# Windowed attention in an AdaLN block: full-array transposes of the probabilities, and a new order of the slot's stages on TensorE, VectorE and ScalarE

## Chip, core and metric

One NeuronCore of a Trainium2 chip runs the whole program in one launch. The metric is the device time of that launch in microseconds (us). The kernel before takes 1208.83 us, the median of 3 runs (1204.72 to 1213.89).

## What is computed

The input is x, 16 sequences of 512 tokens with 128 channels, float32. The part that the change touches is the attention half of the block:

```
h = _layernorm(x, axis=-1) * (1 + ca) + sa
x = x + ga * _L0_attn_ref(h, w_qkv, w_out)

# _L0_attn_ref: H, D, window_size = (16, 64, 32)
xn = rms_norm(x)
q, k, v = jnp.split(xn @ w_qkv.T, 3, axis=-1)     # then split in 16 heads of 64
q = apply_rope(q, cos, sin)
k = apply_rope(k, cos, sin)
attn = jnp.einsum('bhqd,bhkd->bhqk', q, k) * scale
mask = (q_pos >= k_pos) & (q_pos - k_pos <= window_size)
attn = softmax(where(mask, attn, NEG))
out = jnp.einsum('bhqk,bhkd->bhqd', attn, v)
return out.transpose(0, 2, 1, 3).reshape(B, T, H * D) @ w_out.T
```

The second half (a second modulated layer norm, a dense attention over the 16 sequences, a mixture of 8 experts with one expert per token, two more layer norms) is the function `phase2`. The change does not touch it.

## The kernel before, in words

Everything is float32. A projection with a weight is done as three matmuls in the type fp32r, on a high and a low part of both operands: high by high, low by high, high by low.

The attention half runs as a software pipeline over 128 items, 16 sequences ("blocks") times 8 pairs of heads. The loop variable `s` counts slots, 137 of them. In slot `s` each engine works on several items at once, each at another stage. The offsets are `LS, LE, LT, LV, LO, LY = 2, 3, 4, 5, 6, 9` (line 166): the stage with offset L handles item `s - L`. The order of the stages inside a slot is written out by hand for each engine, and each engine takes its instructions strictly in that order. Semaphores say when operands and buffers are ready.

In one slot of the kernel before, TensorE does in this order:

1. q and k of item s: six matmuls 128x512 (lines 322 to 324, twice), into the two banks `PJ`. This is "rope" in the plan of the banks.
2. Scores of item s-2 (line 336): for 8 windows of 64 queries and both heads, 64 queries by 96 keys, into the banks `SC`.
3. Transposes of the probabilities of item s-4 (line 351): 16 transposes of 64 queries by 96 keys, so that the keys lie on partitions, into the banks `TR`. Those of the queries on partitions 0 to 63 go to one bank, those of 64 to 127 to the other. The two kinds stand in turn.
4. Probabilities by values ("PV") of item s-5 (line 367), into the bank `OB`.
5. Once in a block: four transposes of the finished output `yt` (line 377), and in another slot four of the next block's normed input `xn` (line 287), both full 128x128.
6. Values of item s (lines 298 to 300): three matmuls 128x512.
7. Output projection of item s-6 (lines 392, 393, 395): three matmuls 128x512 that accumulate in the bank `ACC` over the 8 items of a block.

ScalarE does in a slot: 8 exponentials (line 681, item s-3, with row sums), two copies of the transposed probabilities to SBUF (`pT`, line 691, item s-4), the copy `oth` of the PV result (line 700, item s-5) and the copy `vn` of the values (line 713, item s). Once in a block it adds four squares (line 647, slot 3), four scalings (line 654, slot 5) and the copy `xh` (line 662, slot 6).

VectorE does four multiplications by cos and sin from PSUM (lines 511, 512, item s), 8 masked row minima of the scores (line 523, item s-2), a reciprocal (line 532, item s-3) and the low part `otl` of the PV result (line 549, item s-5). Once in a block it adds the copy `yt` (line 501), `x1` (line 542), `xl` (line 429), the statistics (lines 411, 416) and, at the end of slot 1, `centre` (line 423): four instructions `(x - mean) * rstd`, each 128x128.

GpSimd adds the two halves of rope (`qk`, line 615, item s-1) and multiplies the exponentials by the reciprocals (line 621, item s-3). In some slots it adds a part of the next block's layer norm (lines 574 to 594) or the residual (line 635). SyncE issues the DMAs that swap partitions for rope (`sw`, line 221, four in a slot) and that spread the values over the windows (`vw`, lines 231 to 234).

Two banks `PJ` are used in turn by rope (two uses in a slot), values, `xn` and `yt`. So the second rope projection of slot s+1 waits for `vn` of slot s, and the first one for the second pair of cos and sin products of slot s.

## Time and profile before

| what | value |
|---|---|
| median of 3 runs | 1208.83 us |
| the profiled execution's own time | 1204.72 us |
| its span | 1202.7 us |
| TensorE busy | 1070.0 us, 89% of the span |
| VectorE, ScalarE, GpSimd busy | 971.2, 928.0, 854.8 us |
| mean granted TensorE clock | 0.939 of full speed |

The profiled execution is the fastest of the three. The span runs from the first to the last instruction and leaves 2 us around it. Busy time of TensorE is modelled, since matmuls overlap, so the length of a stretch of matmuls is read from starts, not from the sum of their durations. Releasers are inferred from semaphores.

### The profile page before, as it was taken

What the parts mean: (1) busy time and instruction counts of PE and PEld (TensorE: products, weight loads), DVE (VectorE), ACT (ScalarE), POOL (GpSimd) and SP (SyncE); (2) the same over time, 40 slices, a digit from 0 to 9 for tenths busy, and PEclk for the clock granted to TensorE, in tenths of its full rate; (3) what the DMA queues carried; (4) which work ended last, traced back from release to release, by engine and by line L of the source; (5) the groups of instructions that cost most, each with busy time, mean ns of one, the idle gap of its engine ahead of it and who ended that gap; (6) DMA issues with size and microseconds to landing.
All of it is one profiled execution on the core that took longest, in us unless ns stands there. A gap on an engine that the chain in (4) does not pass through costs nothing. (4 is left out here: it accounts for less than half of the span.)

```text
span 1202.7 us, 51645 instructions
## 1 busy us (share of the span) xinstructions
PE 1070.0 (89%) x18513; PEld 861.0 (72%) x18513; DVE 971.2 (81%) x4190; ACT 928.0 (77%) x3404; POOL 854.8 (71%) x685
## 2 busy tenths in 40 slices
PE   4799999999999999999999999847998985399994
PEld 2577777777777777777777777725877774388883
DVE  6899998898998898989989986636887864278885
ACT  2799989999999899999899997926876753266662
POOL 2787877877878877878778776654566767157777
PEclk7999999999999999999999998969998976599997
DMA  6776766776766666667677667443242212676200
GB/s 198 207 182 166 179 171 165 179 178 171 180 171 168 178 167 171 177 162 185 171 172 183 161 162 186 105 136 130 64 127 98 76 69 107 193 199 177 85 32 31
DMA packets 111034, 181.01 MB, mean 150 GB/s; under 512 B 19726, under 2 KB 64177, under 8 KB 110656
## 3 DMA queue, kind: packets, MB, share of 16 engines
q1 hardware_dynamic: 102944, 158.53, 51.1%
q0 software_dynamic: 6400, 16.82, 3.9%
q8 instruction: 152, 2.49, 0.9%
q10 hardware_dynamic: 1440, 2.36, 0.8%
q14 instruction: 98, 0.80, 0.2%
HBM read 35.20 MB, written 24.73 MB: 50 GB/s over the span
## 5 line engine op out<-in xcount | busy, mean ns | idle before, releaser
L615 POOL TENSOR_TENSOR qk<-mm,sw 128x1024 f32<-128x1024 f32 x128 | 306.2, 2392 | 127.9 <-DMA sw<-mm 127.7
L681 ACT ACTIVATE pr<-sm,mn 128x96 f32<-128x96 f32 x1024 | 368.0, 364 | 1.0 <-DVE mn L523 1.0
L511 DVE TENSOR_TENSOR mm<-bank,cos 128x512 f32<-128x512 f32 x256 | 174.8, 683 | 47.9 <-PE bank L324 40.9
L621 POOL TENSOR_TENSOR pr<-pr,ri 128x768 f32<-128x768 f32 x128 | 189.1, 1477 | 28.7 <-DVE ri L532 28.4
L681 ACT ACTIVATION_READ_ACCUMULATOR pr<-sm,mn 128x1 f32 x1024 | 195.3, 191 | 0.0
L523 DVE CUSTOM_DVE_ANT_0 sm<-bank,msk 128x96 f32<-128x96 f32 x1024 | 191.0, 252 | 2.3 <-PE bank L336 2.3
L512 DVE TENSOR_TENSOR mm<-bank,sin 128x512 f32<-128x512 f32 x256 | 174.3, 681 | 0.0
L691 ACT ACTIVATE pT<-bank 96x512 f32<-96x512 f32 x256 | 137.1, 586 | 24.8 <-PE bank L351 18.6
L367 PE MATMUL bank<-pT,vw 96*64 96x64 f32 x4096 | 149.1, 226 | 0.0
L367 PEld LDWEIGHTS bank<-pT,vw 96*64 96x64 f32 x4096 | 131.3, 139 | 10.3 <-issue 0.7
L336 PEld LDWEIGHTS bank<-qk 64*64 64x64 f32 x4096 | 90.9, 133 | 59.2 <-issue 56.6
L336 PE MATMUL bank<-qk 64*64 64x96 f32 x4096 | 114.7, 250 | 11.9 <-POOL qk L615 11.7
L1285 ACT ACTIVATE fv<-bank,b1t 128x128 f32<-128x128 f32 x288 | 82.4, 368 | 52.2 <-PE bank L1146 51.4
L322 PE MATMUL bank<-xh,wh 128*128 128x512 f32 x256 | 106.0, 414 | 8.9 <-DVE xl L429 5.7
L713 ACT ACTIVATE vn<-bank 128x512 f32<-128x512 f32 x128 | 76.2, 596 | 48.1 <-PE bank L300 46.2
L549 DVE TENSOR_TENSOR otl<-bank,oth 128x512 fp32r<-128x512 f32 x128 | 84.9, 664 | 26.3 <-ACT oth L700 26.1
L324 PE MATMUL bank<-xh,wl 128*128 128x512 f32 x256 | 102.1, 399 | 0.0
L323 PE MATMUL bank<-xl,wh 128*128 128x512 f32 x256 | 101.9, 398 | 0.0
L992 POOL DMA_INDIRECT out<-h,rr x72 | 76.9, 1068 | 30.5 <-issue 27.0
L351 PE MATMUL bank<-ident,pr 64*96 64x64 f32 x2048 | 83.8, 222 | 9.5 <-POOL pr L621 9.4
L987 POOL DMA_INDIRECT sorted_scratch<-rr,slot x64 | 64.9, 1014 | 29.9 <-issue 17.6
L523 DVE DVE_READ_ACCUMULATOR2_ANT mn<- 128x1 f32 x1024 | 85.3, 83 | 0.0
(206 smaller groups left out, 2484.2 us busy)
## 6 DMA issues: line engine op xcount, KB each, us to landing
sw<-mm SPq DMA_DIRECT2D x512, 128.0 KB, 2.4
vw<-vn SPq DMA_DIRECT2D x128, 192.0 KB, 2.6
vw<-vn SPq DMA_DIRECT2D x128, 128.0 KB, 2.4
rr<-sorted_scratch SPq DMA_DIRECT2D x72, 192.5 KB, 2.8
vw<-vn SPq DMA_DIRECT2D x96, 64.0 KB, 2.6
xt<-in_x SPq DMA_DIRECT2D x16, 256.0 KB, 4.0
x_scratch<-x SPq DMA_DIRECT2D x16, 256.0 KB, 2.6
rr<-x_scratch SPq DMA_DIRECT2D x16, 256.0 KB, 2.9
```

Source lines behind the costliest of these rows:

```text
L322: pe.matmul(dst[:, :], wh[:, o:o + P], xh[b % 2][:, :], start=True, stop=False)
L323: pe.matmul(dst[:, :], wh[:, o:o + P], xl[b % 2][:, :], start=False, stop=False)
L324: pe.matmul(dst[:, :], wl[:, o:o + P], xh[b % 2][:, :], start=False, stop=True).then_inc(s_pj, 1)
L336: ins = pe.matmul(SC[h][64 * e:64 * e + 64, p * WK:(p + 1) * WK], t[r, 0, 32 + 64 * w:96 + 64 * w], t[r, 1, 64 * w:64 * w + WK], start=Tru ...
L367: ins = pe.matmul(OB[64 * h:64 * h + 64, 64 * w:64 * w + 64], vw[half % 2][:, w, c:c + 64], pT[i % 2][:, h, 64 * w:64 * w + 64], start=Tru ...
L511: dve.tensor_tensor(mm[s % 2][:, 0, j, :], PJ[u % 2][:, :], cos[:, :], ALU.mult)
L512: dve.tensor_tensor(mm[s % 2][:, 1, j, :], PJ[u % 2][:, :], sin[:, :], ALU.mult)\
L523: ins = dve.tensor_tensor_reduce(ms_[i % 2][:, h, p, :], SC[h][:, p * WK:(p + 1) * WK], msk[:, min(p, 1), :], 1.0, 3.0e38, ALU.add, ALU.mi ...
L615: pool.tensor_tensor(qk[i % 2][:, :, 32:], mm[i % 2][:, 0, :, :], sw[i % 2][:, :, :], ALU.add)\
L621: pool.tensor_tensor(t, t, ri[i % 2][:, :].unsqueeze(2).to_broadcast([P, 8, WK]), ALU.mult)\
L681: ins = act.activation(pr[i % 2][:, h, p, :], ms_[i % 2][:, h, p, :], ACT.Exp, scale=-1.0, bias=mn[i % 2][:, h, p:p + 1], accum_out=sums[i ...
L691: act.activation(pT[i % 2][:, :, :].rearrange("k h (p e q) -> k (h p) e q", p=4, e=2)[:, :, e, :], TR[e][0:WK, :].rearrange("k (a q) -> k ...
```

## The change

Three things change, all in the attention half.

The probabilities are transposed by 8 full transposes of 128 queries by 96 keys in place of 16 of 64 by 96. There is a bank `TR` for each head now, and `pT` is written in one straight run in place of pieces of 64.

The order of the stages inside a slot is another. TensorE: rope (s), output projection (s-6), scores (s-2), the block's `yt` and `xn`, PV (s-5), values (s), transposes (s-4). ScalarE: the copies `pT` stand at the head of the slot, of item s-5, the others follow as before. VectorE: the copy `yt` moves from the head of the next slot to behind `xl`, and the reciprocal from before `xl` to just before `otl`. The offsets are unchanged.

`centre` becomes a `tensor_scalar` with two scalars per partition, without the broadcast operand.

```diff
@@ TensorE: the output projection (s - LO), unchanged in itself, now stands here, after rope
+                    i = s - LO
+                    if 0 <= i < NI:
...
                     i = s - LS
...
-                    i = s - LT
-                    if 0 <= i < NI:
-                        pe.wait_ge(s_nm, i + 1)
-                        if i == 0:
-                            pe.wait_ge(s_hm, 2)
-                        else:
-                            pe.wait_ge(s_te, 2 * i)
-                        for p in range(4):
-                            for h in range(2):
-                                for e in range(2):
-                                    r, o = slice(64 * e, 64 * e + 64), 256 * h + 64 * p
-                                    ins = pe.transpose(TR[e][0:WK, o:o + 64], pr[i % 2][r, h, p, :], ident[r, r])
-                                    if p == 3 and h == 1:
-                                        ins.then_inc(s_tr, 1)
+                    i = s - LY
...
+                    if s < NI and s % G == 6 and s // G + 1 < NB:
+                        to_columns(s // G + 1)
                     i = s - LV
...
                     if s < NI:
                         values(s)
-                    i = s - LO
+                    i = s - LT
                     if 0 <= i < NI:
+                        pe.wait_ge(s_nm, i + 1)
+                        if i == 0:
+                            pe.wait_ge(s_hm, 2)
+                        for h in range(2):
+                            if i:
+                                pe.wait_ge(s_te, 2 * i - 1 + h)
+                            for p in range(4):
+                                ins = pe.transpose(TR[h][0:WK, p * P:(p + 1) * P], pr[i % 2][:, h, p, :], ident[:, :])
+                            ins.then_inc(s_tr, 1)
@@ VectorE, centre
-                        ins = dve.scalar_tensor_tensor(out=hh[:, j, :], in0=xt[b % 4][:, j, :], scalar=mv[:, j, 0:1],
-                                                       in1=lnr[:, j:j + 1].to_broadcast([P, C]), op0=ALU.subtract, op1=ALU.mult)
+                        ins = dve.tensor_scalar(hh[:, j, :], xt[b % 4][:, j, :], mv[:, j, 0:1], lnr[:, j:j + 1],
+                                                ALU.subtract, ALU.mult)
@@ VectorE, the copy yt: from the head of the slot (i = s - LO - 1) to behind x_low (i = s - LO)
-                    i = s - LO - 1
...
+                    i = s - LO
+                    if 0 <= i < NI and i % G == G - 1:
+                        b = i // G
+                        dve.wait_ge(s_op, i + 1)
...
@@ ScalarE: at the head of the slot, before the exponentials
+                    i = s - LV
+                    if 0 <= i < NI:
+                        if i >= 2:
+                            act.wait_ge(s_pv, i - 1)
+                        for h in range(2):
+                            act.wait_ge(s_tr, 2 * i + h + 1)
+                            act.activation(pT[i % 2][:, h, :], TR[h][0:WK, :], ACT.Copy).then_inc(s_te, 1)
...
-                    i = s - LT
-                    if 0 <= i < NI:
-                        if i >= 2:
-                            act.wait_ge(s_pv, i - 1)
-                        for e in range(2):
-                            act.wait_ge(s_tr, 2 * i + e + 1)
-                            act.activation(pT[i % 2][:, :, :].rearrange("k h (p e q) -> k (h p) e q", p=4, e=2)[:, :, e, :],
-                                           TR[e][0:WK, :].rearrange("k (a q) -> k a q", q=64), ACT.Copy).then_inc(s_te, 1)
```

In the order of the program the lines of the changed kernel have other numbers: 334, 335, 337 are the output projection, 350 the scores, 377 PV, 392 the transposes, 676 the copies `pT`, 685 the exponentials, 696 `oth`, 709 `vn`. Lines 298 to 300 and 322 to 324 keep theirs.

TensorE of the kernel before, from the end of rope to the output projection of the same slot. Names: `qk` and `xh`, `wh` are operands of scores and projections, `pr` the probabilities, `bank` any PSUM bank.

```order
L324 MATMUL bank<-xh,wl 128x512
L336 MATMUL bank<-qk 64x96 [waits a_add,a_mx]
L336 MATMUL bank<-qk 64x96 x15
L351 MATMUL bank<-ident,pr 96x64 [waits a_te,a_nm]
L351 MATMUL bank<-ident,pr 96x64 x15
L367 MATMUL bank<-pT,vw 64x64 [waits a_te,a_ol,a_ot]
L367 MATMUL bank<-pT,vw 64x64 x15
L298 MATMUL bank<-wh,xh 128x512 [waits a_rope]
L299 MATMUL bank<-wl,xh 128x512
L300 MATMUL bank<-wh,xl 128x512
L392 MATMUL bank<-oth,woh 128x512 [waits a_ot]
```

TensorE of the changed kernel, from the end of the output projection to the first rope matmul of the next slot, in a slot with the block's `xn`:

```order
L337 MATMUL bank<-otl,woh 128x512 [waits a_ol]
L350 MATMUL bank<-qk 64x96 [waits a_add,a_mx]
L350 MATMUL bank<-qk 64x96 x15
L287 MATMUL bank<-ident,xn 128x128 [waits a_xn,a_rope]
...
L377 MATMUL bank<-pT,vw 64x64 [waits a_te,a_ol,a_ot]
L377 MATMUL bank<-pT,vw 64x64 x15
L298 MATMUL bank<-wh,xh 128x512 [waits a_rope]
...
L392 MATMUL bank<-ident,pr 96x128 [waits a_te,a_nm]
L392 MATMUL bank<-ident,pr 96x128 x3
L392 MATMUL bank<-ident,pr 96x128 [waits a_te]
L392 MATMUL bank<-ident,pr 96x128 x3
L322 MATMUL bank<-xh,wh 128x512 [waits a_xl]
```

The transposes moved from behind the scores to behind the values, and the output projection from behind the values to before the scores. In a slot of the old order the twelve fp32r matmuls stand in one run; in the new one there are nine, then the values' three by themselves.

ScalarE of the kernel before, one slot (`sm`, `mn` are the masked scores and their minima):

```order
L681 ACTIVATE pr,sums<-sm,mn 128x96 [waits a_ri,a_tr,a_mx]
L681 ACTIVATE pr,sums<-sm,mn 128x96 x3
L681 ACTIVATE pr,sums<-sm,mn 128x96 [waits a_mx]
...
L691 ACTIVATE pT<-bank 96x8x64 [waits a_tr,a_pv]
L691 ACTIVATE pT<-bank 96x8x64 [waits a_tr]
L700 ACTIVATE oth<-bank 128x512 [waits a_op,a_pv]
L713 ACTIVATE vn<-bank 128x512 [waits a_vd1,a_pj]
```

ScalarE of the changed kernel, one slot:

```order
L676 ACTIVATE pT<-bank 96x512 [waits a_tr,a_pv]
L676 ACTIVATE pT<-bank 96x512 [waits a_tr]
L685 ACTIVATE pr,sums<-sm,mn 128x96 [waits a_ri,a_tr,a_mx]
L685 ACTIVATE pr,sums<-sm,mn 128x96 x3
L685 ACTIVATE pr,sums<-sm,mn 128x96 [waits a_mx]
...
L696 ACTIVATE oth<-bank 128x512 [waits a_op,a_pv]
L709 ACTIVATE vn<-bank 128x512 [waits a_vd1,a_pj]
```

The copies `pT` moved from behind the exponentials to before them and belong to the transposes of the slot before.

## Rows read from the trace of the kernel before

**Rows 1.** The page: span, and the granted clock over 40 equal slices.

```profile
span 1202.7 us, 51645 instructions
...
PEclk7999999999999999999999998969998976599997
```

**Rows 2.** Busy time, granted clock and DMA share in the steady stretch of the attention half.

```profile
core 0: us, PE busy (x) PEld busy (x) DVE busy (x) ACT busy (x) POOL busy (x), PEclk, DMA share, GB/s
100.00:750.00 650.00, 631.25 (x10326) 499.69 (x10325) 581.71 (x2640) 598.48 (x2398) 506.92 (x314) 0.99 0.69 173
```

**Rows 3.** VectorE's copy `yt`, once in a block, from 100 to 750 us.

```profile
L501 DVE COPY yt<-bank x13: 691/692/694, 145.8 to 703.9; 128x512 f32<-128x512 f32 x13
```

**Rows 4.** Waits, all engines, 100 to 750 us: total, times, longest.

```profile
POOL qk L615 <- DMA sw<-mm: 105.0, 81, 6.0
...
PE bank L336 <- POOL qk L615: 6.7, 8, 2.5
PE bank L351 <- POOL pr L621: 5.2, 13, 0.4
```

**Rows 5.** TensorE in order of time: start us, us, line, names, shapes.

```profile
441.24 0.66 PE L377 MATMUL bank<-ident,yt 128*128 128x128 f32 x4
441.65 0.48 PE L298 MATMUL bank<-wh,xh 128*128 128x512 f32 x1
441.97 0.39 PE L299 MATMUL bank<-wl,xh 128*128 128x512 f32 x1
...
443.14 0.39 PE L322 MATMUL bank<-xh,wh 128*128 128x512 f32 x1
...
444.31 0.40 PE L324 MATMUL bank<-xh,wl 128*128 128x512 f32 x1
444.63 0.89 PE L336 MATMUL bank<-qk 64*64 64x96 f32 x32
445.45 0.65 PE L351 MATMUL bank<-ident,pr 64*96 64x64 f32 x16
446.04 1.15 PE L367 MATMUL bank<-pT,vw 96*64 96x64 f32 x32
447.12 0.50 PE L298 MATMUL bank<-wh,xh 128*128 128x512 f32 x1
447.46 0.40 PE L299 MATMUL bank<-wl,xh 128*128 128x512 f32 x1
```

**Rows 6.** Four full float32 transposes elsewhere in the program, and one's duration in ns.

```profile
816.16 0.60 PE L1036 MATMUL bank<-ident,h 128*128 128x128 f32 x4
...
L1036 PE MATMUL bank<-ident,h x64: 269/273/446, 802.9 to 967.0; 128*128 128x128 f32 x64
```

**Rows 7.** VectorE, GpSimd and TensorE in order of time, around `centre`.

```profile
354.24 2.45 DVE L423 SCALAR_TENSOR_TENSOR hh<-xt,mv,lnr 128x128 f32<-128x128 f32 x4
...
358.41 0.68 DVE L512 TENSOR_TENSOR mm<-bank,sin 128x512 f32<-128x512 f32 x1
...
354.50 1.52 POOL L621 TENSOR_TENSOR pr<-pr,ri 128x768 f32<-128x768 f32 x1
...
359.63 2.40 POOL L615 TENSOR_TENSOR qk<-mm,sw 128x1024 f32<-128x1024 f32 x1 [1.52 <-DMA sw<-mm]
...
364.64 2.41 POOL L615 TENSOR_TENSOR qk<-mm,sw 128x1024 f32<-128x1024 f32 x1
...
362.18 0.89 PE L336 MATMUL bank<-qk 64*64 64x96 f32 x32 [0.81 <-POOL qk L615]
363.51 0.65 PE L351 MATMUL bank<-ident,pr 64*96 64x64 f32 x16 [0.45 <-POOL pr L621]
```

**Rows 8.** `centre` and a `tensor_scalar` of the same form: duration ns min/median/max.

```profile
L423 DVE SCALAR_TENSOR_TENSOR hh<-xt,mv,lnr x64: 338/345/2482, 6.7 to 683.3; 128x128 f32<-128x128 f32 x64
...
L1480 DVE TENSOR_SCALAR h<-h,xmv,xrs x72: 334/342/540, 1059.3 to 1193.8; 128x128 f32<-128x128 f32 x72
```

**Rows 9.** ScalarE in order of time, a lap in which it waits for nothing.

```profile
371.15 1.06 ACT L691 ACTIVATE pT<-bank 96x512 f32<-96x512 f32 x2
...
372.58 0.59 ACT L713 ACTIVATE vn<-bank 128x512 f32<-128x512 f32 x1
...
375.93 1.07 ACT L691 ACTIVATE pT<-bank 96x512 f32<-96x512 f32 x2
```

More of the change, by code:

```diff
@@ L324, in _ @@
                             pe.matmul(dst[:, :], wl[:, o:o + P], xh[b % 2][:, :], start=False, stop=True).then_inc(s_pj, 1)
+                    i = s - LO
+                    if 0 <= i < NI:
+                        b, g = divmod(i, G)
+                        pe.wait_ge(s_ot, i + 1)
+                        if i == 0:
+                            pe.wait_ge(s_woh, 2)
+                            pe.wait_ge(s_wol, 2)
+                        if g == 0 and b:
+                            pe.wait_ge(s_yt, b)
+                        pe.matmul(ACC[:, :], woh[:, g, :], oth[i % 2][:, :], start=(g == 0), stop=False, skip_group_check=True)
+                        pe.matmul(ACC[:, :], wol[:, g, :], oth[i % 2][:, :], start=False, stop=False, skip_group_check=True)
+                        pe.wait_ge(s_ol, i + 1)
+                        pe.matmul(ACC[:, :], woh[:, g, :], otl[i % 2][:, :], start=False, stop=(g == G - 1),
+                                  skip_group_check=True).then_inc(s_op, 1)
                     i = s - LS
@@ L494, in _ @@
                 for s in range(SLOTS):
-                    i = s - LO - 1
-                    if 0 <= i < NI and i % G == G - 1:
-                        b = i // G
-                        dve.wait_ge(s_op, i + 1)
-                        if b:
-                            dve.wait_ge(s_pj, pj_use[("yt", b - 1)] + 1)
-                        dve.tensor_copy(yt[:, :], ACC[:, :]).then_inc(s_yt, 1)
                     for j in range(2):
@@ L543, in _ @@
                                           mod[:, b:b + 1, 2 * C:].to_broadcast([P, 4, C]), ALU.mult).then_inc(s_y, 1)
+                    i = s - LE
+                    if 0 <= i < NI:
+                        dve.wait_ge(s_exp, 2 * i + 2)
+                        if i >= 2:
+                            dve.wait_ge(s_nm, i - 1)
+                        dve.reciprocal(ri[i % 2][:, :], sums[i % 2][:, :]).then_inc(s_ri, 1)
                     i = s - LV
```

39 lines of the change are left out of this document (12 added, 27 removed).

## The prediction, made before the changed kernel was run

> **What bounds the kernel now.** I read the page first. The granted clock is 9 tenths or more in slices 2 to 25 of 40, so one long even stretch fills two thirds of the 1202.7 us [rows 1]. The busy times of that stretch come next: in the 650 us from 100 on, TensorE is busy 631.25 us, ScalarE 598.48, VectorE 581.71, GpSimd 506.92, at a granted clock of 0.99, which is the 2.4 GHz level [rows 2]. Four engines are near their limit there, so which of them sets the pace is not to be had from shares.
>
> The pace itself is read from something that happens once in a block of 8 slots. The copy `yt` starts 13 times from 145.8 to 703.9 us, so a block takes (703.9 - 145.8) / 12 = 46.51 us and a slot 5.81 [rows 3].
>
> Then I laid out one slot of TensorE from the starts in order of time [rows 5]. From the first rope matmul at 443.14 to the scores at 444.63 it takes 1.49 us. The six matmuls in it are 0.234 apart (443.14 to 444.31 is five of them), and the last, before the scores, takes 0.32. Scores: 0.82. Transposes: 445.45 to 446.04, 0.59. PV: 1.08. Of the six fp32r matmuls that follow, the first takes 0.34 (447.12 to 447.46) and the other five 0.234 each. Sum: 1.49 + 0.82 + 0.59 + 1.08 + 0.34 + 1.17 = 5.49 us; I use 5.48. So the first fp32r matmul behind a float32 group costs 0.1 more than its neighbours, and the last one before such a group 0.09 more.
>
> A block needs 8 x 5.48 us plus two groups of four full transposes (`yt`, `xn`) at 441.65 - 441.24 = 0.41 each, 44.66 us in all. It takes 46.51. So TensorE is the bound, with 1.85 us of waits in a block. The waits seen are those for `qk` and for the normalised probabilities [rows 4], and rows 7 show where both come from: `centre` takes 2.45 us on VectorE, the rope products behind it end only at 359.09, and one slot later TensorE stands 0.81 us for `qk` and 0.45 us for `pr`. The rest are a late `vn` and a late `xl` in slots 5 and 6.
>
> **The change part by part.**
>
> *Transposes.* 16 half transposes go and 8 full ones come. The old ones stand in turn on the upper and lower half of the array's rows and run two at a time: 0.59 us for all. The new ones fill all rows, so nothing runs beside them. The trace has no 128x96 one, but it has full ones: four take 0.60 us from first start to last end, and one lasts 0.273, so they start (0.60 - 0.273) / 3 = 0.109 us apart [rows 6]. Four cost 0.41 us [rows 5], eight 0.41 + 4 x 0.109 = 0.85 us. That is 0.26 us more in each slot. The bounds: 0.59, if the narrower weights made them as cheap as the pairs, and 0.87 (8 x 0.109). I take 0.85. The group of 16 has the same 96 columns of weights, so narrower weights are in the old price already.
>
> *Order on TensorE.* The twelve fp32r matmuls are split into nine and three. This adds one change into float32 (values to transposes, 0.09) and one back (transposes to rope, 0.32 instead of 0.234, as 441.65 to 441.97 shows [rows 5]). Sum 0.18 us a slot. Bounds: 0 and 0.2; I take 0.18.
>
> The new slot: nine matmuls 8 x 0.234 + 0.32 = 2.19; scores 0.82; PV 1.08; values 0.34 + 0.234 + 0.32 = 0.89; transposes 0.85; the first rope matmul's extra 0.09. Sum 5.92 us, against 5.48. The block's own transposes stay at 0.41 each.
>
> *Waits on TensorE, one by one in the new slot* (time from its first rope matmul). The projection starts at 1.4 and needs `oth`, `otl` of the slot before; VectorE ends `otl` at about 5.5 of its 5.92, so 1.8 us of slack. The scores start at 2.2 instead of 1.5. `qk` needs 8.0 us from the end of the rope products (359.09) to its own end (364.64 + 2.41) [rows 7]. Those products end at about 3.3, and the scores come two slots later, 2 x 5.92 + 2.2 - 3.3 = 10.7 us on. Slack 2.7 us. The transposes start at 5.0 and need `pr`, which GpSimd ends about 1 us into the slot: 4 us of slack. PV starts at 3.0 and needs `pT`, now copied at the head of ScalarE's slot and ended by 0.9. All waits of before have got more room, so I count all 1.85 us of a block as gone.
>
> *ScalarE.* The copies are made earlier in its slot and the exponentials about 1 us later; behind the exponentials wait `oth`, `vn`, the reciprocal and `otl`. A lap without waits takes 375.93 - 371.15 = 4.78 us [rows 9], against 5.92. The mean load with the block's work is 598.48 us over 650 / 5.81 = 112 slots, 5.35 us. That leaves 0.57 us a slot on average, 1.1 in a plain slot, and `vn` is needed 0.8 us after it is ready. A lump (squares, about 2 us) is taken up without a wait on TensorE, just. Price 0; if the cover is too thin it is part of the old 1.85 us. A straight `pT` in place of pieces of 64: the old one takes 0.53 a copy (1.06 for two) [rows 9], the straight `vn` 0.59. No gain.
>
> *`centre`.* Unheld, an old instruction takes 0.345 us; the longest 2.482. In rows 7 the group of four takes 2.45 us while GpSimd runs `pr` (354.50 to 356.02): one of them is held until GpSimd is done. The new form is in the trace in the second half, 0.342 us, longest 0.540 [rows 8], so about 1.1 us for four and 1.3 us saved in a block on VectorE. It lies beside TensorE's work, so it is worth something only through the waits that are already counted as gone. The Trainium skill, page "SBUF — State Buffer", section "Who interferes with whom", says that `tensor_scalar` can enter a mode with two ports, and then contends with GpSimd, which would block it fully. By that rule `centre` would stay at 2.45 us. No row here has this form beside a GpSimd operation on tensors, so the trace leaves it open. If it is held, the rope products come 1.1 us later in slot 2, less than the 2.7 us of slack, and the sum stands.
>
> *Copy `yt`, reciprocal.* Same work, and each is still ahead of who needs it. Price 0, bounds -0.2 and +0.2 us a block.
>
> *Sum.* Slots: 128 x (5.92 - 5.48) = +56.3 us. Waits of the 14 inner blocks: 14 x 1.85 = -25.9 us. In the first and last block TensorE waits for the fill and for a queue of DMAs; the wider slack takes up perhaps 4 us, an estimate from the 0.7 us by which the scores come later and the 0.44 us of each slot. -4. Total +26.4 us. The second half and the drain are unchanged. From the profiled execution's own 1204.72 us this gives 1231.1; from the median, 4.1 us above it, 1235.2. I forecast 1233 us.
>
> **Rivals.**
>
> *A. The switches and the wider transposes cost less than the rows say.* If the extra changes between fp32r and float32 cost nothing, 128 x 0.18 = 23 us fall away: 1210 us. For it: the old 0.34 stands behind PV, whose small tiles may be its cause. Against it: behind four full transposes it is still 0.32.
>
> *B. The waits stay.* ScalarE's lap starts with copies of transposes that TensorE makes last in its slot, right behind the values. If squares and scalings push `pT`, `oth` and `vn` so far that TensorE waits in slots 4 to 7 as before, the 26 us do not come back: 1259 us; with half of them, 1246. For it: ScalarE is loaded 5.35 of 5.92 us. Against it: the slack above.
>
> *C. Faster: TensorE's pace isn't raised.* The one mechanism is that 8 full transposes pass in the 0.59 us of the 16 half ones and the switches are free, so that a slot stays at 5.48 and the waits go: 1208.8 - 30 = 1179 us. It decides from the point at which the eight cost 0.26 us less than rows 5 and 6 say. For it: the number of instructions is halved. Against it: 0.109 us between full transposes in two places, and twice as many columns stream when no two share the rows.
>
> *D. `centre` is held as before, and the slack isn't there.* Then the scores of one slot in eight wait up to 1.3 us: 15 x 1.3 = 20 us more, 1253 us. It is counted under B. The page's rule named above speaks for it.
>
> **How the numbers follow.** The forecast gets 0.62, A 0.13, B with D 0.19, C 0.06. About 1% is what a measurement of this kernel can tell from no change, 1197 to 1221 us here. The forecast and B are slower, A is within, C is faster: 0.81, 0.13, 0.06. The range goes from A's 1210 to between B's half and whole, 1255.
>
> **What would show it.** A block of the changed kernel should take 8 x 5.92 + 0.82 = 48.2 us from one `yt` to the next. On TensorE eight transposes should take 0.85 us, start to next start, and two starts of fp32r behind float32 should be seen in a slot. The rows "L336 <- POOL qk" and "L351 <- POOL pr" of the waits should have next to nothing that answers to them, and ScalarE's and VectorE's idle shares should rise. `centre` should take 1.1 us if it is free of GpSimd, 2.45 if not, with no effect on the block. I am wrong if eight transposes take under 0.7 us, if a block is under 47 us, or if TensorE is idle more than 0.5 us in a block.

## The result, and the profile after

| | before | changed |
|---|---|---|
| median | 1207.5 us (1202.0 to 1213.89, 9 runs) | 1218.9 us (1211.6 to 1222.47, 9 runs) |
| profiled execution, own time | 1204.72 us | 1215.93 us |
| its span | 1202.7 us | 1213.9 us |

The ratio is 1.0084, with a 95% interval from 1.0054 to 1.0113. The change makes the kernel slower, and by less than the forecast: 11 us and not about 25. That is on the near side of the 1% that the prediction called no change, a case to which it gave 0.13.

The page of the changed kernel, span, busy times and granted clock:

```profile
span 1213.9 us, 49597 instructions
...
PE 1102.0 (91%) x17489; PEld 901.6 (74%) x17489; DVE 971.9 (80%) x4190; ACT 921.6 (76%) x3404; POOL 854.2 (70%) x685
...
PEclk9899999999999999999999999969898886599997
```

The even stretch answers to [rows 2]:

```profile
100.00:750.00 650.00, 650.00 (x9357) 528.39 (x9356) 576.10 (x2618) 588.20 (x2376) 500.77 (x311) 1.00 0.68 170
```

By the profile's modelled busy time TensorE is now busy for all of the 650 us, where before it was busy for 631.25. The three other engines have each lost a little, because fewer slots fit in. The granted clock is 1.00, still the 2.4 GHz level, so the clock explains nothing of the difference.

The copy `yt`, which answers to [rows 3], gives the pace:

```profile
L525 DVE COPY yt<-bank x13: 684/689/690, 146.4 to 713.2; 128x512 f32<-128x512 f32 x13
```

A block takes (713.2 - 146.4) / 12 = 47.23 us against 46.51, so 0.72 us more. Fourteen inner blocks make 10.1 us of the 11.2 by which the spans differ. The second half is unchanged (443.1 us after the last slot, 443.0 before).

The waits, 100 to 750 us, answer to [rows 4]:

```profile
POOL qk L612 <- DMA sw<-mm: 72.1, 67, 3.8
POOL pr L618 <- DVE ri L540: 61.1, 66, 2.1
DVE mm L501 <- PE bank L324: 49.6, 69, 1.1
...
ACT oth L696 <- PE bank L377: 37.7, 70, 1.0
...
PEld bank L322 <- ACT vn L709: 2.6, 13, 0.2
```

No row is left in which TensorE waits for `qk` or `pr`. VectorE and ScalarE wait for TensorE more than before: VectorE for the rope banks, ScalarE for the PV bank. From one first rope matmul to the next, the eight slots of a block take 6.34, 5.76, 5.75, 5.75, 5.75, 5.8, 6.35 and 5.76 us. A plain slot is 5.75, the two with the block's own transposes are 0.59 longer, and 8 x 5.75 + 2 x 0.59 = 47.18 leaves 0.05 us of waits in a block. Before, the same list was 5.88, 5.48, 5.48, 5.8 to 7.0, 5.48, 5.95, 6.35, 5.58: a plain 5.48, and waits in slots 3, 5 and 6 and a little in 7.

One slot of TensorE in order of time, as in [rows 5]:

```profile
368.22 0.39 PE L337 MATMUL bank<-otl,woh 128*128 128x512 f32 x1
368.54 0.89 PE L350 MATMUL bank<-qk 64*64 64x96 f32 x32
369.36 1.15 PE L377 MATMUL bank<-pT,vw 96*64 96x64 f32 x32
370.44 0.50 PE L298 MATMUL bank<-wh,xh 128*128 128x512 f32 x1
370.78 0.39 PE L299 MATMUL bank<-wl,xh 128*128 128x512 f32 x1
371.01 0.39 PE L300 MATMUL bank<-wh,xl 128*128 128x512 f32 x1
371.24 1.04 PE L392 MATMUL bank<-ident,pr 128*96 128x128 f32 x8
372.03 0.47 PE L322 MATMUL bank<-xh,wh 128*128 128x512 f32 x1
372.34 0.39 PE L323 MATMUL bank<-xl,wh 128*128 128x512 f32 x1
```

Read the gaps between starts. The last projection matmul takes 0.32 before the scores, and the first values matmul 0.34 behind PV: these are the two raised gaps that [rows 5] also has. The last values matmul takes 0.23 before the transposes, the ordinary gap, although fp32r meets float32 there. The transposes take 0.79 and the first rope matmul 0.31, which is 0.08 above the ordinary 0.23. Together 0.79 + 0.08 = 0.87 = 8 x 0.109, the transposes' own cadence: the matmul behind them starts 0.08 early and gives it back. So nothing at all is added where the type changes.

What costs is something else. The rows give the part of the array that a matmul uses, rows times columns: 64\*64 for the scores, 96\*64 for PV, 64\*96 for the old half transposes. These are the small tiles, with at most 64 rows or at most 64 columns. fp32r matmuls (128\*128) and full transposes (128\*128 for `yt` and `xn`, 128\*96 for the probabilities) count as the whole array here, since no gap is raised between them. From the whole array to small tiles the gap before the group is 0.09 us longer than the ordinary one, and behind the first matmul on the way back it is 0.10 longer. The block's own transposes show that the tile matters. In [rows 5] they stand behind PV, beside other work on the whole array, and take 0.41. Now they stand between scores and PV, both in small tiles:

```profile
350.69 0.89 PE L350 MATMUL bank<-qk 64*64 64x96 f32 x32
351.51 0.66 PE L360 MATMUL bank<-ident,yt 128*128 128x128 f32 x4
352.10 1.15 PE L377 MATMUL bank<-pT,vw 96*64 96x64 f32 x32
```

Here they take 352.10 - 351.51 = 0.59, so 0.18 more. The Trainium skill, page "TensorEngine Tiling (Array Packing)", section "Key Properties", says that a change of tiling mode drains TensorE, and not a change of tile. It gives no price. The trace agrees, with the 0.09 and 0.10 us above; the 16 half transposes alternate between two tiles of one size, and their starts stay evenly 0.056 us apart in pairs.

VectorE and GpSimd around `centre`, which answer to [rows 7]:

```profile
360.30 2.26 DVE L420 TENSOR_SCALAR hh<-xt,mv,lnr 128x128 f32<-128x128 f32 x4
...
360.43 1.54 POOL L618 TENSOR_TENSOR pr<-pr,ri 128x768 f32<-128x768 f32 x1
```

```profile
L420 DVE TENSOR_SCALAR hh<-xt,mv,lnr x64: 332/338/2406, 6.5 to 692.8; 128x128 f32<-128x128 f32 x64
```

The four instructions last 338, 1494, 334 and 336 ns. The second ends within 0.1 us of GpSimd's `pr`. So `tensor_scalar` is held by a GpSimd operation on tensors just as the old form was, and unheld it is hardly shorter (338 ns against 345). The group takes 2.26 us against 2.45.

### The profile page after: what moved, and what is told of

The parts are those of the page before. It is cut to its first block and busy times, and to the rows that moved or that the text cites. A ratio compares the mean times of both kernels' runs of the same rounds, so it can differ in the third digit from the quotient of the medians.

```text
span 1213.9 us, 49597 instructions
## 1 busy us (share of the span) xinstructions
PE 1102.0 (91%) x17489; PEld 901.6 (74%) x17489; DVE 971.9 (80%) x4190; ACT 921.6 (76%) x3404; POOL 854.2 (70%) x685
## 5 line engine op out<-in xcount | busy, mean ns | idle before, releaser
L685 ACT ACTIVATION_READ_ACCUMULATOR pr<-sm,mn 128x1 f32 x1024 | 202.0, 197 | 0.0
L392 PE MATMUL bank<-ident,pr 128*96 128x128 f32 x1024 | 132.7, 273 | 0.0
L392 PEld LDWEIGHTS bank<-ident,pr 128*96 128x96 f32 x1024 | 115.6, 126 | 18.9 <-issue 0.2
L322 PE MATMUL bank<-xh,wh 128*128 128x512 f32 x256 | 113.6, 444 | 1.9 <-DVE xl L426 1.4
L696 ACT ACTIVATE oth<-bank 128x512 fp32r<-128x512 f32 x128 | 76.2, 596 | 48.0 <-PE bank L377 48.0
```

The lines of the kernel that those rows point to most:

```text
L322: pe.matmul(dst[:, :], wh[:, o:o + P], xh[b % 2][:, :], start=True, stop=False)
L392: ins = pe.transpose(TR[h][0:WK, p * P:(p + 1) * P], pr[i % 2][:, h, p, :], ident[:, :])
L685: ins = act.activation(pr[i % 2][:, h, p, :], ms_[i % 2][:, h, p, :], ACT.Exp, scale=-1.0, bias=mn[i % 2][:, h, p:p + 1], accum_out=sums[i ...
```

## Experiments

Two theories of the slot were put to the chip. T: a slot pays 0.19 us for each run of small-tile work (0.09 in, 0.10 out), and type changes are free. D: the slot grows only by the longer transposes, and where they stand is free. Both give 5.75 for the changed kernel, so its own profile can't tell them apart. A block is always read from the first and last start of the copy `yt`, as in [rows 3].

The first four (e1, e2, e3, e8) ran on one chip, beside the kernel before at 1204.91 us. The others ran on three other chips, where the kernel before takes 1247 to 1249 us. In most traces from there the part behind the last slot takes 41 to 55 us longer than the 443 us above (488 in e9, 494 in e7). The first half is the same (the changed kernel's block was 47.23 in e15 too). So they are judged by blocks and slots, and their ratios are each against the kernel before beside them. The kernel before was not traced there, and its slot 3 varies from block to block, so differences of 0.2 us between blocks of the old order say little by themselves.

### The slot

**e1: the kernel before, with full transposes in the old place.**

```diff
-                        for p in range(4):
-                            for h in range(2):
-                                for e in range(2):
...
-                                    ins = pe.transpose(TR[e][0:WK, o:o + 64], pr[i % 2][r, h, p, :], ident[r, r])
+                        for h in range(2):
...
+                            for p in range(4):
+                                ins = pe.transpose(TR[h][0:WK, p * P:(p + 1) * P], pr[i % 2][:, h, p, :], ident[:, :])
```

> The kernel before with the 8 full transposes alone, in their old place between scores and PV; the order of all stages is the old one. Theory T (what costs extra on TensorE is a change between matmuls on the full array and matmuls on 64 or 96 of its rows or columns, whatever their type): the transposes become a full group between two small-tile groups, as the four of yt are in the changed kernel, 0.59 us. Eight take 0.59 + 4 x 0.109 = 1.03 us from first start to the start of PV, a slot without waits takes 5.48 - 0.59 + 1.03 = 5.92 us. Theory D (the extra is paid between fp32r and float32, as the prediction had it): 0.85 us and a slot of 5.74. Waits partly go with the longer slot; a block of 48.2 to 49 us under T, 46.8 to 48 under D, against 46.5 before; ratio to before 1.02 to 1.03 under T, 1.005 to 1.015 under D.

1234.73 us, ratio 1.0276 (1.0217 to 1.0335). TensorE in order of time:

```profile
400.33 0.89 PE L336 MATMUL bank<-qk 64*64 64x96 f32 x32
401.15 1.08 PE L349 MATMUL bank<-ident,pr 128*96 128x128 f32 x8
402.16 1.15 PE L364 MATMUL bank<-pT,vw 96*64 96x64 f32 x32
```

The transposes take 402.16 - 401.15 = 1.01 us where the 16 half ones took 0.59 and where 8 x 0.109 is 0.87. The plain slot is 5.90. T holds (it said 5.92), D does not (5.74). The extra beyond 8 x 0.109 is 0.14 us, a little less than T's 0.19. The block, from the `yt` row below, is (730.7 - 102.5) / 13 = 48.32. Since 8 x 5.90 + 2 x 0.41 = 48.02, only 0.30 us of waits are left, and nothing in the order was changed. So 1.55 of the old 1.85 us go without a new order; with nothing else changed but the form of `pT`, the longer TensorE slot, which gives the other engines more time, is the likely reason.

```profile
L498 DVE COPY yt<-bank x14: 690/690/692, 102.5 to 730.7; 128x512 f32<-128x512 f32 x14
```

**e2: the changed kernel, with the 16 half transposes in the new place.**

```diff
-                                ins = pe.transpose(TR[h][0:WK, p * P:(p + 1) * P], pr[i % 2][:, h, p, :], ident[:, :])
...
+                                    ins = pe.transpose(TR[e][0:WK, o:o + 64], pr[i % 2][r, h, p, :], ident[r, r])
```

> The changed kernel with the 16 half transposes in place of the 8 full ones, in the new order. Theory T: the half transposes stand alone between two full-array groups (values and rope) and pay an entry of 0.09 and an exit of 0.10 us, so 0.59 + 0.19 = 0.78 us in place of 0.87; a slot of 5.66 us, a block of 46.5 if no waits come back, ratio to before 1.00. Theory D: the changes of type are paid in the 5.75 us of the changed kernel already, so the full 0.28 us come back, a slot of 5.47 and a block of 45.0, ratio to before 0.98.

1212.68 us, ratio 1.0057 (1.0026 to 1.0088).

```profile
409.16 0.39 PE L300 MATMUL bank<-wh,xl 128*128 128x512 f32 x1
409.48 0.65 PE L394 MATMUL bank<-ident,pr 64*96 64x64 f32 x16
410.06 0.50 PE L322 MATMUL bank<-xh,wh 128*128 128x512 f32 x1
410.40 0.39 PE L323 MATMUL bank<-xl,wh 128*128 128x512 f32 x1
```

```profile
L528 DVE COPY yt<-bank x13: 685/685/687, 145.3 to 707.2; 128x512 f32<-128x512 f32 x13
```

The half transposes are small tiles. Between matmuls on the whole array they raise the gap before them to 0.32 and the one behind to 0.34. They themselves take 0.58 as ever. The plain slot is 5.66, as T says. The block is (707.2 - 145.3) / 12 = 46.83. This splits the change: the new order alone costs 46.83 - 46.51 = 0.32 us a block, and the full transposes within it 47.23 - 46.83 = 0.40, though their 0.09 a slot makes 0.72; the difference is waits that were still there at 5.66 (0.37 us) and are gone at 5.75.

**What the price hangs on.** T gets these kernels right and is still too narrow, as single starts in the same traces show. Inside a group the starts are evenly spaced: on average 0.0206 us for each of 32 scores, 0.0292 for each of 32 PV matmuls, 0.0279 for each of 16 half transposes, 0.109 for each of 8 full ones and 0.233 for each of 12 fp32r matmuls. The table adds up a plain slot at these paces and compares it with the measured one.

| | paces alone | measured | difference | changes of tile in the slot |
|---|---|---|---|---|
| before | 4.84 us | 5.48 us | 0.64 us | 4 |
| changed | 5.25 us | 5.75 us | 0.50 us | 3 |
| e1 | 5.27 us | 5.90 us | 0.63 us | 4 |
| e2 | 4.84 us | 5.66 us | 0.82 us | 5 |

That is 0.16 to 0.17 us for each change of tile, those between two kinds of small tile included: before, the first half transposes start 0.17 us behind the last scores, in [rows 5] hidden in the scores' 0.82. The four transposes of `yt` between scores and PV fit as well: 4 x 0.109 = 0.44, one change more is 0.15, and they take 0.59. T counts only the changes out of the whole array and back, and leaves the others in the groups' own 0.82, 0.59 and 1.08. So the two parts of the change can't be priced apart. With half transposes the new order adds a change and costs 0.18 us a slot (e2). With full ones it saves a change and gains 0.15 (5.90 in e1, 5.75 in the changed kernel; the block 48.32 and 47.23).

**e8 and e3: `centre` apart.** e8 is the changed kernel with the old `centre`; e3 is the kernel before with the new one.

```diff
-                        ins = dve.scalar_tensor_tensor(out=hh[:, j, :], in0=xt[b % 4][:, j, :], scalar=mv[:, j, 0:1],
...
+                        ins = dve.tensor_scalar(hh[:, j, :], xt[b % 4][:, j, :], mv[:, j, 0:1], lnr[:, j:j + 1],
```

> The changed kernel with the old centre. The new order leaves slack for a late rope product, so the form of centre makes no difference: slots stay at 5.75 us, a block at 47.2, ratio to before as the changed kernel's, 1.008. Rival (the slack is thin): a wait of TensorE comes back in slot 3, 0.1 to 0.2 us a block, ratio 1.010.

> The kernel before with centre alone as tensor_scalar. Theory H (it is held by GpSimd's running operation like the old form): four instructions take 2.2 to 2.4 us instead of 2.45, the waits in slot 3 stay but for 0.1 to 0.2 us, ratio to before 0.996 to 1.0. Rival: free of GpSimd, 1.1 us for four, the waits for qk and pr in slot 3 (0.4 to 1.5 us a block) go, ratio 0.985 to 0.99.

e8: 1215.62 us, ratio 1.0094 (1.0064 to 1.0123), block (712.7 - 146.1) / 12 = 47.22. e3: 1201.94 us, ratio 0.9984 (0.9955 to 1.0014), block (701.2 - 99.4) / 13 = 46.29; the group still takes 2.32 us, with one instruction of 1507 ns. The form of `centre` has no effect on the changed kernel, and none that can be told apart from nothing on the one before.

### The order

**e4: the changed kernel, with `yt` and `xn` behind PV again, as before.**

```diff
-                    i = s - LY
-                    if 0 <= i < NI and i % G == G - 1:
...
                     i = s - LV
...
+                    i = s - LY
+                    if 0 <= i < NI and i % G == G - 1:
```

> The changed kernel with the block's yt and xn transposes moved from before PV to behind it, so that they stand next to the values again. Theory T: each group of four costs 0.41 us as before the change, not 0.59 as between scores and PV; slots 0 and 6 take 6.16 instead of 6.34, a block 46.86 instead of 47.24, 16 x 0.36 = 6 us less than the changed kernel, ratio to before 1.003 to 1.005. Rival (the 0.59 come from something else in these slots, a bank or a late operand): 47.2 stays, ratio 1.009.

1254.4 us, ratio 1.0076 (1.003 to 1.0122).

```profile
396.75 1.15 PE L367 MATMUL bank<-pT,vw 96*64 96x64 f32 x32
397.83 0.66 PE L377 MATMUL bank<-ident,yt 128*128 128x128 f32 x4
398.24 0.48 PE L298 MATMUL bank<-wh,xh 128*128 128x512 f32 x1
```

```profile
L525 DVE COPY yt<-bank x13: 685/687/689, 145.6 to 709.6; 128x512 f32<-128x512 f32 x13
```

The group is back at 398.24 - 397.83 = 0.41, its slot at 6.14 (6.34 in the changed kernel), and the block at (709.6 - 145.6) / 12 = 47.00. The slot with `xn` fell to 6.27 and not as far: its transposes of the probabilities take 0.92 us up to rope and not 0.79, and rope starts at 434.86, just behind the end of `xl` at 434.80. This is a better form of the change by 0.23 us a block, which the whole time, with its interval, neither shows nor denies, and still slower than the kernel before.

**e5: the changed kernel with half transposes between scores and PV, so that all small tiles are one run. e6: the kernel before, with the output projection alone moved in front of the scores.** Both keep TensorE's own work at 5.48 us a slot. The edit shown is the one of e6 against the kernel before.

```diff
+                    i = s - LO
+                    if 0 <= i < NI:
...
+                        pe.matmul(ACC[:, :], woh[:, g, :], otl[i % 2][:, :], start=False, stop=(g == G - 1),
...
                     i = s - LS
```

> All the small-tile work in one run and all full-array work in another, with ScalarE's and VectorE's new order: rope, output projection, scores, 16 half transposes, PV, yt and xn, values. Theory T and the slack theory (outputs projection before scores and copies pT at the head of ScalarE's slot are what removed the waits): slots of 5.48 us with few waits, a block of 44.7 to 45.3 against 46.5, ratio to before 0.977 to 0.987. Rival (the waits went only because the slot was longer than what ScalarE, 5.35 us, and VectorE, 5.24 us, need with the block's work): waits come back in slots 1 to 7, a block of 46 to 46.5, ratio 0.993 to 1.0.

> The kernel before with one move alone: the output projection of s-6 behind rope instead of behind the values. Scores and half transposes come 0.7 us later than the rope product that they need. If that slack alone takes up the wait behind centre, the 0.4 to 1.5 us of slot 3 go and a block takes 45.3 to 45.8, ratio to before 0.985 to 0.995; the waits of slots 5 and 6 (0.46 us each, for vn and xl) stay. Rival: they get worse, since the second rope product now follows the values with 0.7 us less in between, waits of 0.7 us in each slot for vn, a block of 47 or more, ratio over 1.01.

Both missed. e5: 1285.36 us, ratio 1.0326 (1.0219 to 1.0434), block (729.6 - 99.7) / 13 = 48.45. e6: 1277.99 us, ratio 1.0241 (1.0102 to 1.038), block (727.7 - 101.3) / 13 = 48.18. A plain slot takes 5.73 in both, and 5.58 where `yt` or `xn` was in the slot ahead; slots 4 and 5 of e5 have further waits (5.97 and 6.15). TensorE of e6 at the turn of a slot, and the rows of waits of e6 and of e5 that belong to it:

```profile
402.84 0.40 PE L324 MATMUL bank<-xh,wl 128*128 128x512 f32 x1
403.23 0.50 PE L322 MATMUL bank<-xh,wh 128*128 128x512 f32 x1
403.56 0.39 PE L323 MATMUL bank<-xl,wh 128*128 128x512 f32 x1
```

```profile
PEld bank L322 <- ACT vn L713: 42.4, 80, 1.1
```

```profile
PEld bank L322 <- ACT vn L713: 39.6, 80, 0.9
```

The second rope projection stands 0.39 us behind the last matmul of the first one, in place of 0.23, and the gap behind its own first matmul is 0.33 and not 0.23 as well: together the 0.25 us of the slot. It needs the bank that ScalarE empties with `vn`, and with the projection gone from behind the values there is too little ahead of it. The row of before is 8.1 us, 13 times; here it is 42.4 and 39.6, 80 times, in six slots of eight. In the changed kernel the transposes stand behind the values and are that cover (2.6 us, 13 times). So the split of the small tiles, which costs 0.18 in e2, can't be had back by this shift. In e6 slot 3's wait for `qk` is gone in nearly every block. The scores come 0.7 us later there, as the prediction argued, but the slot is also 0.25 us longer, and in e5, with the same two, slot 3 still takes 5.7 to 6.6 us. So what the later scores do by themselves isn't shown.

### Where the old waits came from

**e7: `centre` cut to a quarter.** From the second block on it leaves out three of the four instructions, the held one among them, so the normalised input is incomplete there.

```diff
-                    for j in range(4):
+                    for j in range(4 if b == 0 else 1):
```

> The kernel before, in which centre does only the first of its four instructions from the second block on (the norm of three quarters of the rows is left out there, so the output is not the reference's). This takes 2.1 us of VectorE away, the 1.2 us of being held among them, and leaves TensorE its work. If the wait in slot 3 comes from centre, slot 3 falls from 5.8 to 7.0 us to 5.48 and a block to 45.6 to 45.8, ratio to before 0.985 to 0.99; the waits of slots 5 and 6 stay. Rival (the wait comes from the landing of the DMAs in any case): slot 3 stays over 5.8.

1249.92 us, ratio 1.0021 (0.9976 to 1.0067), block (703.0 - 99.5) / 13 = 46.42. Slot 3 still takes 5.5 to 6.9 us, 6.2 in the mean of 13 blocks, against 6.3 before. The prediction named `centre` as the source of that wait, and it is not.

**e9: the block's two 256 KB transfers issued four slots later** (SyncE issues the store of `x` and the load of `xt` just ahead of the four partition swaps of rope).

```diff
-                    if s >= LY and (s - LY) % G == G - 1:
-                        b = (s - LY) // G
+                    b = (s - LY) // G if s == SLOTS - 1 else (s - LY - 4) // G
+                    if s == SLOTS - 1 or b in range(NB - 1) and (s - LY - 4) % G == G - 1:
```

> The kernel before with the two 256 KB transfers of a block (x1 out, x in; lines 255 and 188) issued four slots later, after the same instructions of VectorE. Theory Q (the wait of slot 3 for qk comes from these transfers: they are issued ahead of the rope swaps of slot 1, which then land late; centre is not its cause, since a quarter of centre left it): slot 3 falls to 5.48 to 5.6 us and a like wait may come up around slot 7; a block of 45.7 to 46.5, ratio to before 0.985 to 1.0. Rival (GpSimd's own block work in slots 0 to 2, 1.3 to 2.6 us in each, is the cause): slot 3 stays at 5.7 to 7 us.

1245.52 us, ratio 0.9989 (0.9961 to 1.0018), block:

```profile
L501 DVE COPY yt<-bank x14: 691/692/692, 99.5 to 700.0; 128x512 f32<-128x512 f32 x14
```

(700.0 - 99.5) / 13 = 46.19, 0.32 less than before. Slot 3 falls to 5.57 to 5.95; in four blocks slot 4 rises to 6.3 to 6.9 in its place. So the transfers in front of the swaps make part of slot 3's wait. The trace of the kernel before shows the same order on SyncE:

```profile
352.20 0.38 SPq L255 DMA_DIRECT2D x_scratch<-x  x1
352.62 0.51 SPq L188 DMA_DIRECT2D xt<-in_x  x1
353.23 2.42 SPq L221 DMA_DIRECT2D sw<-mm  x4
...
359.12 2.48 SPq L221 DMA_DIRECT2D sw<-mm  x4
```

The `qk` that starts at 359.63 in [rows 7], after 1.52 us for a swap, is the one that follows the four swaps issued from 353.23 on. Its rope products ended at 352.24, ahead of `centre` (354.24). The products behind `centre`, which end at 359.09, are swapped only from 359.12 on and go into the next `qk`, at 364.64. So the order of the rows that the prediction had before it already spoke against `centre` as the source of this wait.

**e11: ScalarE's four squares split over slots 3 and 4, and scaling, `xh`, `xl`, `xn` one slot later. e12: e11 and e9 together.**

```diff
...
                         if r == 3:
-                            squares(b)
-                        if r == 5:
+                            squares(b, (0, 1))
+                        if r == 4:
+                            squares(b, (2, 3))
+                        if r == 6:
                             scaled(b)
```

> The kernel before with ScalarE's block work spread: two squares each in slots 3 and 4 instead of four in slot 3, and what follows (reciprocal root on GpSimd, scalings, xn, xh, xl) one slot later. The lump theory (the 0.46 us of slot 5 are the four squares, 1.7 us, which ScalarE's 0.7 us of slack in a 5.48 us slot cannot take up): slot 5 falls from 5.95 to 5.5, the wait for xl moves from slot 6 to slot 7 with the same 0.46 us; a block 0.4 us shorter, 46.0, ratio to before 0.993 to 0.997. Rival: slot 5 stays, and the kernel is the same within 0.3%.

> The two edits of the last two together. If the causes are two separate ones, their gains add: a block of 45.2 to 45.8 us against 46.5, ratio to before 0.98 to 0.99, which beats both kernels. If the late transfers only push the wait to slot 7, where the wait for xl is now too, 46 us and 0.993.

e11: 1249.33 us, ratio 0.9991 (0.9948 to 1.0034), block (702.2 - 99.7) / 13 = 46.35. Its profiled execution, at 1258.68 us, was one of its longer ones. Slot 5 is at 5.48, so its 0.47 us came from the squares: in the kernel before, the exponentials of slot 4 stand behind them on ScalarE, then `vn`, for which TensorE waits in slot 5. The gain doesn't reach the block. Slots 6 and 7 keep their length together (6.35 + 5.58 before, 5.48 + 6.44 here, where `xn` has gone to slot 7), and slots 0 and 1 take 6.15 and 5.58 in place of 5.88 and 5.48. e12: 1252.42 us, ratio 1.006 (1.0017 to 1.0102), block (705.6 - 145.5) / 12 = 46.68. The two gains do not add: the wait turns up in other slots. A block of the old order sits at 46.2 to 46.7 us whatever is lightened.

**e10: the kernel before, with ScalarE's copies `pT` at the head of its slot** (half transposes, TensorE's order as before).

```diff
+                    i = s - LV
+                    if 0 <= i < NI:
...
+                            act.wait_ge(s_tr, 2 * i + e + 1)
...
                     i = s - LE
...
-                    i = s - LT
-                    if 0 <= i < NI:
```

> The kernel before with one move alone: the copies pT at the head of ScalarE's slot, for the transposes of the slot before. TensorE keeps its order and its 5.48 us. Theory: slot 3's wait for qk is not touched; the slots 5 and 6 wait for vn and xl as before, since both still come behind the exponentials; a block of 46.5, ratio to before 0.995 to 1.005. Rival (the copies at the head are what removed the waits): slots 3, 5 and 6 fall to 5.5 to 5.9, a block of 45, ratio under 0.985.

1257.26 us, ratio 1.0113 (1.0048 to 1.0179), block (706.0 - 100.2) / 13 = 46.60. Slot 3's waits stay, and the 0.46 us of slot 5 are now in slot 4. By the block ScalarE's new order gives nothing by itself. The ratio is larger than 0.1 us a block explains; the block is read from the shortest of only four executions (1248.02 us), and this is left open.

### Looking for a better order

**e13: the changed kernel with the values right behind rope and the projection, and half transposes between scores and PV**, so that `vn` has cover and the small tiles are one run. ScalarE makes `vn` right behind the exponentials there, ahead of `oth`, and `yt` stands behind PV. **e14: the same with e9's transfers.**

```diff
+                    if s < NI:
+                        values(s)
                     i = s - LS
...
+                                    ins = pe.transpose(TR[e][0:WK, o:o + 64], pr[i % 2][r, h, p, :], ident[r, r])
...
                     i = s - LV
...
-                    if s < NI:
-                        values(s)
```

> A new order with 16 half transposes: TensorE does rope, output projection, values, then scores, half transposes, (xn,) PV, (yt); ScalarE does pT, exponentials, vn, xh, oth. All full-array matmuls stand in one run and all small-tile ones in another, scores come 1.4 us later than in the kernel before, and vn has the whole small-tile run (2.5 us) as cover. Theory T plus the slack theory: slots of 5.48 us, no wait for vn or qk, xn between small tiles at 0.59 and yt at 0.41: a block of 44.9 to 45.3 against 46.48 before and 47.19 in the changed kernel, 17 to 22 us less than before, ratio to before 0.981 to 0.988. Rival (ScalarE, 5.35 us with the block's work against a mean slot of 5.6, or VectorE becomes the bound): waits of 1 us or more a block come back, for oth or otl, a block of 46 or more, ratio 0.995 or more.

> The same with the two 256 KB transfers of a block issued four slots later. If the slack of the new order already covers the late rope swaps, there is no difference to the run before, within 0.2 us a block; if slot 3 keeps a wait there, it goes.

e13: 1365.62 us, ratio 1.0944 (1.0899 to 1.099), block (711.8 - 106.4) / 11 = 55.04. e14: 1371.66 us, ratio 1.0987 (1.094 to 1.1033), block (712.3 - 107.2) / 11 = 55.01, so the transfers make no difference. Waits of e13, 100 to 750 us, and one of them in order of time:

```profile
PEld bank L298 <- DVE mm L505: 110.4, 93, 2.9
...
ACT oth L708 <- PE bank L385: 121.1, 71, 3.8
```

```profile
444.85 0.50 PE L298 MATMUL bank<-wh,xh 128*128 128x512 f32 x1 [0.23 <-DVE mm L505]
```

The values now take the bank just after rope, and must wait until VectorE has made the cos and sin products from it. VectorE has `otl` ahead of these products, `otl` waits for `oth`, and `oth` for PV, which now stands behind the waiting values. It is a loop through three engines, and each turn costs TensorE 0.6 us and more: a plain slot takes 6.07. Slot 2 takes 9.5 to 10.8, and there two things come together:

```profile
521.66 0.79 PE L298 MATMUL bank<-wh,xh 128*128 128x512 f32 x1 [2.45 <-DVE mm L505]
522.25 0.63 PE L299 MATMUL bank<-wl,xh 128*128 128x512 f32 x1
522.68 0.63 PE L300 MATMUL bank<-wh,xl 128*128 128x512 f32 x1
```

```profile
522.00:535.00 13.00, 13.00 (x176) 10.29 (x176) 7.32 (x41) 5.65 (x22) 7.41 (x4) 0.64 0.44 109
```

VectorE has `centre` ahead of the products, 2.20 us from 518.21 on, and TensorE stands idle for 2.45 us. Behind the idle time the granted clock is 0.64 over 13 us, part of them at the 1.2 GHz level, and the fp32r matmuls start 0.43 us apart in place of 0.23. In other blocks the stretch is shorter (0.60 from 303 to 307 us). So in this order `centre` does reach TensorE, and a stall is paid for twice.

**e15: the changed kernel again, beside these.**

> The changed kernel itself, on the chip of the two runs before it, for their comparison: a block of 47.2 us, ratio to before 1.007 to 1.01.

1255.59 us, ratio 1.0053 (1.0021 to 1.0086), block (711.9 - 145.2) / 12 = 47.23, as on the first chip. No version was found that beats the kernel before by more than the measurement's uncertainty; e3, e9 and e11 lie within it.

## Why the prediction was wrong

The sum was 128 x 0.44 - 25.9 - 4 = +26.4 us. It came to +11.2. None of the three signs by which the prediction would have called itself wrong came up (0.79 us for the transposes, a block of 47.23, 0.05 us of waits in it), so they were too wide to catch its error.

*Transposes: right for the place where they stand now.* +0.26 us was forecast from [rows 6]. It is 0.87 - 0.59 = 0.28, with the cadence of 0.109 that was read there. In the old place, between small tiles, they cost 0.42 (e1).

*Order on TensorE: this is the step that failed.* "This adds one change into float32 (values to transposes, 0.09) and one back (transposes to rope, 0.32 instead of 0.234). Sum 0.18 us a slot." Measured: 0, with transposes at 0.28; against e1, which has the same transposes in the old order, the new order even takes 0.15 off. The 0.34 and 0.32 of [rows 5] were read as the price of the type; the 0.34, and the 0.32 before the scores, are the price of a change of tile (e1, e2, e4). The 0.32 behind four full transposes, which the prediction took as its proof, is the last transpose's own time: it starts at 441.62, the values' first two matmuls at 441.65 and 441.97, and 0.35 us is 0.109 + 0.24. In all the slot was forecast 128 x 0.17 = 21.8 us too long. The prediction had both halves of the right reading in rival A: it named the small tiles as a possible cause, and gave it 0.13.

*The block's own transposes "stay at 0.41 each": wrong.* Between scores and PV they cost 0.59, 0.18 more. For 30 of them that is 5.4 us that the sum lacked. With the right rule both errors would have been seen at once: the move takes one group out from between the small tiles and puts another in.

*Waits: right in size, wrong in part of the cause.* 1.85 us a block went to 0.05 and gave back 1.8 x 14 = 25.2 us against 25.9. But `centre` was not what made slot 3 late (e7, and the order of the swaps in the trace of before); the block's transfers are a part (e9), and slot 5 is the squares' (e11). How the rest of slot 3 divides was not settled. The wider slack of the new order was not needed for most of it either: e1 loses 1.55 of 1.85 us with the old order. So most of the waits were a reserve that a longer stretch of work on TensorE uses up first. Rival B is out.

*ScalarE: right.* No wait on TensorE for `pT` or `oth`, at 588.20 us busy of 650.

*`centre`: wrong, without effect.* 1.1 us was forecast if free of GpSimd; it takes 2.26. The rule that the prediction cited from the Trainium skill, page "SBUF — State Buffer", section "Who interferes with whom", was right in its outcome, since the second instruction is held for 1.16 us beside GpSimd's `pr`; that the instruction was in the mode which the rule names isn't shown, as its unheld 338 ns are hardly shorter than the old form's 345. The row of the second half [rows 8] could not speak against it: 68 of its 72 instructions lie beside a DMA issue of GpSimd (`out<-h,rr`, 1.07 us), none beside a GpSimd operation on tensors, and none lasts over 0.540 us. The price of zero stood, as the prediction said it would in that case (e8).

*Ends: right as far as can be told.* -4 forecast. With 128 slots of 0.27 (34.6), the block's transposes (5.4) and the waits (25.2), the measured 11.2 leaves -3.6. This is a remainder and not a reading of its own, so that the corrected sum comes out is no proof of it.

Corrected, the sum is 34.6 + 5.4 - 25.2 - 3.6 = +11.2 us. The forecast slot of 5.92 and block of 48.2 us are, by chance, nearly those of e1 (5.90, 48.32): there the full transposes do pay 0.14 us extra, near the 0.18 that the prediction put in the wrong place.

## What to carry to other kernels

Sort TensorE's work in a slot by the tile of the array that it uses, and count the changes of tile, those between two small tiles too: each costs some 0.16 us of the slot here, and the type of the operands costs nothing. A group's price so depends on its neighbours, and a new kind of work and a new order have to be priced together. Before an extra gap behind a group is called a price, subtract the group's own last instruction, and look for a second place where the supposed cause stands without the other one. Before a stage is moved, ask which evacuation it was covering; the waits that a longer slot hides are no merit of a new order.

## What was not expected of the hardware

- A change between the tiles 128\*128, 64\*64, 64\*96 and 96\*64 costs 0.16 to 0.17 us of TensorE's time (before, changed, e1, e2). At the ends of an fp32r run it is seen as gaps of 0.32 and 0.34 us between starts, against 0.23. Between fp32r matmuls (128\*128) and full float32 transposes (128\*128 or 128\*96): nothing.
- `tensor_scalar` on 128 float32 elements with two scalars per partition: 338 ns, near the 345 of `scalar_tensor_tensor`, and held for 1.2 us by GpSimd's `tensor_tensor` (after, e3). Beside GpSimd's DMA issues it is not held (68 times in the second half, at most 0.540 us).
- Behind 2.45 us of idle time in a busy stretch the granted clock was 0.64 over the next 13 us (e13).
